# Cross-attention and a routed feed-forward layer: the part after the attention loop in quarters, in another order, with five product tiles

## The reference

```python
# x (1, 1024, 128), ctx (1, 6404, 128), mask (1, 1024, 6404): True hides the key; 16 heads of 8
q, k, v = heads(layernorm(x) @ Wq.T + bq), heads(ctx @ Wk.T + bk), heads(ctx @ Wv.T + bv)
scores = where(mask, finfo.min, q @ k.T / sqrt(8))
x = x + merge(softmax(scores) @ v) @ Wo.T + bo
n = layernorm(x)
probs = softmax(n @ gate_w.T)                  # 8 experts
p, e = top_k(probs, 2)
h = gelu(n @ w1[:, e, :].T + b1[e])            # 512 hidden, for each of the two experts
x = x + sum(p * (h @ w2[:, e, :].T + b2[e]))
```

## Time and profile before

| | us |
|---|---|
| median of 3 runs | 332.46 (331.86 to 334.14) |
| the profiled execution's own time | 330.95 |
| its span, from the first to the last instruction | 329.3 |
| attention loop ends, sums are turned | 214.3 |
| last copy of an expert weight ends | 241.6 |
| first tile from DRAM is multiplied | 273.3 |
| last expert tile's product ends | 316.9 |

### The profile page before, as it was taken

The page is one execution under the profiler, slowest core; times in us unless marked ns, Lnnn a source line. Parts: engine busy times, 40 slices in busy tenths (PEclk is TensorE's granted clock), DMA queues, the critical chain, the costliest instruction groups (busy, mean ns, idle before and its releaser), DMA issues.

```text
span 329.3 us, 6448 instructions
## 1 busy us (share of the span) xinstructions
PE 267.3 (81%) x1941; PEld 134.8 (41%) x1944; DVE 176.7 (54%) x431; ACT 230.0 (70%) x366; POOL 80.5 (24%) x137
## 2 busy tenths in 40 slices
PE   2689978989999989898989898966777577799940
PEld 2455534122121212121222222254666577798940
DVE  4799864354535363535454535476963125677612
ACT  4458856999999999999999999716951212555520
POOL 8891013000000000100010004030387105344430
PEclk9999999999999999999999999999979597999995
DMA  7999580101010101010100101895011521100115
GB/s 214 360 402 404 195 178 6 41 2 40 0 40 12 28 12 28 12 28 14 26 21 19 26 14 28 304 317 89 17 49 51 145 57 35 32 29 30 34 36 187
DMA packets 29011, 29.31 MB, mean 89 GB/s; under 512 B 15341, under 2 KB 22913, under 8 KB 28864
## 3 DMA queue, kind: packets, MB, share of 16 engines
q1 hardware_dynamic: 27536, 26.21, 26.2%
q0 software_dynamic: 1456, 2.86, 2.9%
HBM read 21.62 MB, written 7.45 MB: 88 GB/s over the span
## 4 chain that ended last, share of the span: by engine, by line
PE 45%; ACT 19%; issue 16%; DVE 11%; DMA 3%; another core or an unknown queue 2%; DVEq 2%; ACTq 1%; POOL 0%; POOLq 0%; SPq 0%
PE bank L1385 12%; ACT w2T L1073 10%; PE bank L1367 7%; PE bank L1494 6%; PE bank L1502 3%; PE bank L1235 3%; ACT arenaB L1073 3%; PE bank L1512 2%; PE bank L1196 2%; DVE arenaB L949 1%; PE bank L1261 1%; ACT w1T L1099 1%; ACT w2T L1099 1%; DMA x_sb<-in_x_dram 1%
## 5 line engine op out<-in xcount | busy, mean ns | idle before, releaser
L756 DVE TENSOR_TENSOR arenaA<-bank,arenaA 128x512 f32<-128x512 f32 x80 | 55.2, 691 | 80.0 <-PE bank L1385 80.0
L1073 ACT ACTIVATE arenaB<-bank 128x1024 f32<-128x1024 f32 x80 | 77.5, 1021 | 2.8 <-PE bank L1367 0.7
L1073 ACT ACTIVATE w2T<-bank 128x1024 f32<-128x1024 f32 x80 | 76.6, 1029 | 3.4 <-PE bank L1367 2.9
L1367 PE MATMUL bank<-qS,keys 64*128 64x512 bf16 x328 | 62.7, 386 | 10.7 <-ACT w2T L1073 7.6
L1106 ACT ACTIVATE mask_u<-bank,arenaB 128x128 f32<-128x128 f32 x92 | 26.3, 369 | 46.5 <-PE bank L1494 41.7
L1367 PEld LDWEIGHTS bank<-qS,keys 64*128 64x128 bf16 x328 | 15.5, 92 | 98.0 <-ACT w2T L1073 51.4
L1385 PE MATMUL bank<-arenaB,vcur 128*32 128x512 f32 x320 | 42.6, 604 | 2.8 <-DVE vcur L749 2.6
L1385 PE MATMUL bank<-w2T,vcur 128*32 128x512 f32 x320 | 42.6, 605 | 0.0
L411 POOL CAST keep<-flags 128x1 f32 x12 | 2.3, 189 | 161.1 <-DVE arenaC L649 139.6
L1494 PE MATMUL bank<-arenaB 128*128 128x128 f32 x184 | 28.1, 302 | 10.9 <-DVE arenaB L941 9.9
L1494 PEld LDWEIGHTS bank<-arenaB 128*128 128x128 f32 x184 | 24.7, 209 | 13.2 <-DVE arenaB L941 11.9
(11 more groups left out here) (318 smaller groups left out, 349.0 us busy)
## 6 DMA issues: line engine op xcount, KB each, us to landing
mask_u<-in_L_ffn_w_dram SPq DMA_DIRECT2D x2, 2048.0 KB, 10.5
mask_u<-in_mask_BxSxS_bk_dram SPq DMA_DIRECT2D x6, 560.5 KB, 12.6
ctx_sb<-in_ctx_dram SPq DMA_DIRECT2D x3, 768.0 KB, 13.4
qS<-qparts_dram SPq DMA_DIRECT2D x4, 448.0 KB
mask_u<-in_mask_BxSxS_bk_dram SPq DMA_DIRECT2D x6, 240.0 KB, 10.8
keys_in<-kparts_dram SPq DMA_DIRECT2D x40, 32.0 KB
mask_u<-in_mask_BxSxS_bk_dram SPq DMA_DIRECT2D x1, 1121.0 KB, 7.5
qparts_dram<-arenaA SPq DMA_DIRECT2D x2, 512.0 KB, 8.1
```

The lines of the kernel that those rows point to most:

```text
L756: nc.vector.tensor_tensor(a, bank[:, 4 + k % 2, :], a, ALU.add).then_inc(s["ac"], 1)
L1073: nc.scalar.activation(probs[u % 8], bank[:, 2 * (u % 2):2 * (u % 2) + 2, :].rearrange("p a b -> p (a b)"), ACT.Exp, scale=SCALE).then_inc ...
L1367: last = mm(bank[:, 2 * (u % 2) + a, :], keys[rows, g, :], qS[rows, g, cols], start=not hides, stop=True, tile_position=(64 * a, 0))
```

## The change

- The sums are turned and normalised in four quarters of two tiles (`sums_turn(qd)`, `normalise(qd)`), in other PSUM banks (`U_BANKS`).
- Queries without keys: the flags themselves ([128, 16] per tile) are turned on PE beside the context, and a product of 16 rows (flags times `uniform`) is accumulated on the projection. `uniform` is by head the mean of all values times `wo_x`, made once (`spread`, `by_head`, one product, one copy on ACT).
- Per quarter: `context_turn` (four transposes), one ACT copy of 128x512, `projected` (four products), and DVE's `joined`.
- `expert_weights` moves: the blocks 0 to 3 are turned right behind the projection, the rest behind the ranking products; ACT copies two of them before its square root. The eight row copies (`rows[1]`) go behind the last weight, and the gate's turned rows are copied by ACT instead of DVE. The variance step goes behind the second choice.
- `b2_products` go ahead of the first tile's rows, the addition of b2 to `x2` to the end.
- `FIRST` is 5, the loads `XS_CUTS` are cut anew (first load: tiles 5 to 7), and `stage` of the first two tiles from DRAM is done inside the loop over the first five.
- The spare slots are filled (`xs_dram`, now eight DMAs) by SP between the loops over the partly hidden and over the other key tiles, no longer behind the weights' loads.

```diff
-FIRST = 4
+FIRST = 5
-XS_CUTS = [(FIRST, 6), (0, FIRST), (6, 12), (12, 18), (18, NT)]
+XS_CUTS = [(FIRST, 8), (0, FIRST), (8, 13), (13, 18), (18, NT)]
...
-            with sp.Fori(1, n + 1) as i:
-                key_rows(i, 1, s["kch"], s["kw"], s["kr"], s["kc"])
+            with sp.If(partial):
+                with sp.Fori(1, partial + 1) as i:
+                    key_rows(i, 1, s["kch"], s["kw"], s["kr"], s["kc"])
+            sp.wait_ge(s["fill"], 2)
+            for b, tiles in enumerate(SPARE):
+                sp.dma_start(xs_dram.rearrange("(j s) c -> s j c", s=P)[:, tiles[0]:tiles[-1] + 1:3, :],
+                             fill[:, b:b + 1, :].broadcast_to([P, len(tiles), ROW])).then_inc(s["xs_fill"], 16)
+            with sp.If(n - partial):
+                with sp.Fori(partial + 1, n + 1) as i:
+                    key_rows(i, 1, s["kch"], s["kw"], s["kr"], s["kc"])
...
+            def normalise(qd):
+                dve.wait_ge(s["u_ps"], qd + 1)
+                b = U_BANKS[qd]
+                U = bank[:, b:b + 2, :].rearrange("p t (h c) -> p t h c", c=32)
...
+                nc.vector.tensor_scalar(flag, U[:, :, :, HD], 0.0, None, ALU.is_equal).then_inc(s["u_dve"], 1)
...
+                nc.vector.tensor_tensor(weight, flag, U[:, :, :, HD], ALU.add).then_inc(s["u_dve"], 1)
...
+                nc.vector.reciprocal(inv, weight).then_inc(s["u_dve"], 1)
...
+            def joined(qd):
+                dve.wait_ge(s["at_ps"], qd + 1)
...
+            for qd in range(4):
+                normalise(qd)
+            dve.wait_ge(s["gxr"], 5)
+            for qd in range(4):
+                joined(qd)
...
             for j in range(FIRST):
+                if j + 3 < FIRST:
+                    places(j + 3)
+                stage(j + 2)
                 if j + 2 < FIRST:
-                    stage(j + 2)
                     slot_rows(j + 2)
                 dve.wait_ge(s["yps"], j + 1)
                 nc.vector.tensor_copy(y_first[:, j, :], bank[:, 4 + j % 2, 0:P]).then_inc(s["yacc"], 1)
-            dve.wait_ge(s["b2ps"], 1)
-            nc.vector.tensor_tensor(x2, x2, bank[:, 6:8, :].rearrange("p a (t d) -> p (a t) d", d=D), ALU.add).then_inc(s["b2ps"], 1)
-            stage(FIRST)
-            stage(FIRST + 1)
...
+            def context_turned(qd):
+                act.wait_ge(s["cq_ps"], qd + 1)
+                nc.scalar.activation(turned[:, qd, :], bank[:, 4, :], ACT.Copy).then_inc(s["cq_sb"], 1)
...
+            expert_weights(0, 2)
             act.wait_ge(s["sqrt2"], 1)
...
+            expert_weights(2, 16)
+            for k in range(2):
+                act.wait_ge(s["gT_ps"], k + 1)
+                nc.scalar.activation(epi_e[:, 512 * k:512 * k + 512], bank[0:E, 5 + 2 * k, :], ACT.Copy).then_inc(s["gT_sb"], 1)
...
+            def projected(qd):
+                pe.wait_ge(s["cq_sb"], qd + 1)
+                for t in range(2):
+                    to = bank[:, AT_BANKS[qd], 256 * t:256 * t + D + XE]
+                    mm(to, turned[:, qd, t * P:(t + 1) * P], wo_x, start=True, stop=False)
+                    last = mm(to, turned[0:H, qd, (2 + t) * P:(3 + t) * P], uniform, start=False, stop=True)
+                last.then_inc(s["at_ps"], 1)
...
+            for qd in range(4):
+                context_turn(qd)
+                projected(qd)
+            expert_weights(0, 4)
```

200 lines of the change are left out of this document (100 added, 100 removed).

## The result

The changed kernel takes 343.74 us (median of 4 runs, 342.44 to 345.85) against 332.16 (4 runs, 331.14 to 334.14) of the kernel before on the same chip: ratio 1.035, 95% interval 1.028 to 1.042. The forecast was 327.9, range 320.5 to 335.5, "faster". It is wrong in sign. The profiled execution took 343.92 us, its span is 342.1 (before 330.95 and 329.3).

What follows compares the result with a forecast made beforehand. It saw PE with idle time in three stretches, ACT filling the weight copies, and PE's notices late beside scatters. Terms +2.1 - 2.9 - 3.8 = -4.6 us gave 326.4 profiled, 327.9 beside the median; range 320.5 to 335.5.

Steps and rivals of the forecast that it cites:

- Step 1, the fills: Attention loop: fills ahead of the first key rows delay the key copy, +2.1 us (bounds 0 to +5).
- Step 2, the quarters: Stage after the attention loop: four serial rounds, about 2.37 us each, start the gate later, +2.6 us (+1 to +4).
- Step 3, the gate: Gate: with the variance step behind the second choice, ACT's square root is no longer hidden, +0.3 us (0 to +0.6).
- Step 4, the weights: Weight copies on ACT: last copy at 240.6 instead of 241.63; tile products start at 243.8 instead of 242.9, +0.9 us.
- Step 5, five tiles: Product tiles: first DRAM tile at 270.4 instead of 273.27, -2.9 us including the quarters, gate and weights.
- I let the notice be as late as before (5.5): Product tiles: PE's completion notice for the third tile's rows stays 5.5 us late, so its copy follows at 256.9.
- rival A: Product tiles: notices come on time, first DRAM tile at 264.9, another -5.5 us, 322.4 in all; chance 0.17.
- rival B: Product tiles: notices held until the scatters end, third up waits until 261.4, 332.4 in all, no change; chance 0.22.
- Step 6, the loop: Loop over tiles from DRAM: one tile fewer (-2.1) and no 1.2 GHz start (-1.7), together -3.8 us.
- C: Product tiles: notices held until scatters end and waiting PE stays at 1.2 GHz for longer, 338.4 us; chance 0.11.
- The signs listed as right or wrong: Trace marks, e.g. right: first key copy near 72, rounds of 2.4 us; wrong: rounds under 2 us, unchanged loop end.

Runs made afterwards that it cites:

- e3: Changed kernel without the 16-row products and the turning and copying of flags for them (output lacks the part for queries without keys): 331.55 us.
- e4: Changed kernel with each quarter's four products reordered, the two of 128 rows first, then the two of 16: 338.64 us.
- e6: Changed kernel with three bf16 products of 512 columns in each pause where PE waits for ScalarE's copy in the rounds: 338.33 us.
- n4: Changed kernel with its 16 indirect scatters of rows made plain transfers of the same bytes (rows unsorted, another output): 333.66 us.
- n2: Kernel before with its 16 indirect scatters of rows made plain transfers (another output): 38.7 us from gate to first DRAM tile instead of 47.3; total not given.
- n1: Kernel before with the 16 scatters of rows held back until the four product tiles are done; its total time is not given in the text.
- h1: Changed kernel with the fills back behind the weights' loads and the stage after the loop in halves, without 16-row products: 329.02 us.
- n3: Kernel before with GpSimd waiting for landing after the fourth, eighth and twelfth scatter of rows: median 323.24 us against 330.16.
- e5: Changed kernel with fills back, 128-row products first, and a second PSUM bank so PE turns the next quarter before projecting this one: 329.41 us.

## Why the prediction was wrong, step by step

*Step 1, the fills: right mechanism, size off.* Predicted +2.1 with bounds 0 to 5, measured +5.2. The queueing was right: the reads were to start 5.8 late and started 7.6 late, since eight fills took 5.58 to issue, not 3.9. The 3.9 came from five loads; the fills' own row in before, seven in 12.54 us beside the weights' loads, was not used. (The 2.1 us from the write's issue to the first read is 2.26 in the earlier trace rows.) The key copy was to start near 71.8 and came at 73.35. Left out was the clock: a starved PE fell to 1.2 GHz for 6.8 us. "ACT is busy 141.25 of 146 us in the loop, so what is lost there is not won back" held.

*Step 2, the quarters: the term that failed most.* Predicted +2.6 (+1 to +4), measured 8.7. The form was right, four serial rounds that PE's queue keeps apart. Two prices in it were wrong. The question "is a product of 16 rows as dear as one of 128?" was put to eight like products in a row and answered with yes, 0.25. That holds for the load itself, but not where row counts alternate: 0.43 each, 3.0 a round instead of 2.37 (e3, e4). And the rounds were priced at full clock, since the trace of before showed no lower one there, which other traces of the same halves do; the halved clock cost 3.7 (e6). 4 x 0.63 = 2.5 and 3.7 make 6.2, against the 6.1 missed. The rule on weight loads was true and beside the point: what bears on it here is the rule on changes of mode, which the prediction did not weigh.

*Step 3, the gate:* gate to Exp 4.89 for 4.52, +0.37; predicted +0.3.

*Step 4, the weights:* right. From Exp to the last copy 7.1 for 11.1, the 4.0 predicted (1.0 and 3.0). The tile products started 3.0 behind it; predicted 3.2.

*Step 5, five tiles: failed at "I let the notice be as late as before (5.5)".* From the gate to the first DRAM tile the sum gave 41.8, rival A 36.3, rival B 46.3; measured 47.3. The lateness is a date, not a length: earlier and more tile products only wait longer (11.4 us at one up). n4, with plain transfers, gives 36.2, which is A's sum to 0.1. So the steps for the engines were about right, though in n4 it is PE's own products from 253.33 on that bind (21.2 us to the first DRAM tile), and not the loads that A names, which left at 257.82; that both gave 264.9 in the prediction was luck. The whole term hung on a mechanism that the prediction had named, priced at 5.5 and given the wrong form. With the order of the change the holding costs 11.1 us (47.3 less n4's 36.2), where before lost 8.6 (n2).

*Step 6, the loop:* predicted -3.8, measured -1.1. The first tiles did run at full clock, as forecast, and a tile was saved, but five scatters of results back to back instead of four held the notices again: PE stood for 1.31 and 2.44 us at 294.00 and 298.60, where before had one wait of 1.67.

*The rivals.* B named the cause behind the gate, to 1 us; it had the third tile's copy as what is held, and in the changed kernel it was already the first tile's gelu, so that two more downs lay behind the release (15.2 us from there to the first DRAM tile, 13.5 in B). C had the sign and the halved clock, but at another place: beside and behind the held notices PE ran at 1.2 GHz for 6.8 and 3.4 us (from 263.3 and from 273.6), as long in all as in before; the long stretch came in the rounds. The signs listed as right or wrong served well: rounds of 2.4 us and the first key copy near 72 both missed, each at a term that was too small.

The fall of the sum is then 3.1 at step 1, 6.1 at step 2, 5.5 at step 5 and 2.7 at step 6: 17.4, from -4.6 to +12.8. With steps 2 and 5 alone put right the sum would be +7.0; with 1 and 6 alone, +1.2, too little to tell from nothing.

## What to carry to other kernels

Price a product between its neighbours: where matmuls of different row counts alternate, group them by row count, and take PE's clock as a term of its own wherever PE works with pauses: one trace at full clock does not say that the next will be. Cut a stage into more rounds only together with a second buffer, so that the next round's first half does not queue behind the last one's second; else each cut adds a copy's latency. A small transfer on the path should not stand behind a bulk one on its queue. And before one moves work ahead to run beside GpSimd's indirect scatters, one should check whether a consumer starts when its producer ends: work won there may only wait longer, while three waits for landing among the scatters, 1.3 us each, took 6.9 us off the median of the kernel before, by taking away its upper level and not by beating the lower one.

## What was not expected of the hardware

- Matmuls' notices of completion are held while GpSimd issues indirect scatters back to back (0.96 us each, 0.30 apart): up to 11.4 us, several of them released together: 1.5 us after the last scatter in before, 2.0 in the changed kernel, 1.1 in n1, but 0.6 ahead of its end in h1. Some come out in the middle of a run, late as well (in before gelus started at 252.54 and 255.45, 3.6 and 4.4 us after their ups), and not every notice within a run of scatters is held (two in n1 came at once). With a wait for landing after every fourth scatter the product tiles' notices came on time (n3). Whether plain transfers do the same, no run shows.
- fp32 products of 137 columns: 0.28 us in a row, 0.33 in pairs of one row count, 0.43 where 128 and 16 rows alternate; the last is 0.76 at 1.2 GHz.
- The granted clock fell to 0.50 in rounds in which PE had 0.69 us of pause in 3.0, and stayed at 1.00 where the pauses were filled (e6), where the stage was over in 10 us (e3) and where there was hardly a pause (e5, PE busy for 11.12 of 11.40). In the stage of two halves it fell in five traces of ten.
- The kernel before has two levels, 8 us apart, in single executions on one chip, and three waits of 1.3 us on GpSimd kept ten of ten on the lower one.
